# A new table of turns for the two streams of a six-layer decoder kernel

## The chip, the cores and the metric

One core of a Trainium2 chip runs the whole program. The metric is the device time of one execution in microseconds (us), from the first to the last instruction and what the runtime adds around it. The engines of the core are PE (matmul), DVE (vector), ACT (activation), POOL (GpSimd) and SP, which here issues every DMA. Each runs its own list of instructions strictly in the order of the list, and they meet only at semaphores.

## The reference

A batch of 16 sequences of 256 tokens with 256 features goes through six sublayers. Each adds its output to its input and normalises the sum:

```python
x = _layernorm(x + mamba(x))             # L0: scan with 512 channels x 16 states, 256 steps
x = _layernorm(x + sparse_latent(x, ctx))  # L0: 16 heads, 64 chosen keys for each query
x = _layernorm(x + bit_ffn(x))           # L0: quantised feed-forward, 256 -> 1024 -> 256, gelu
x = _layernorm(x + self_attention(x))    # L1: 16 heads of 16
x = _layernorm(x + cross_attention(x, ctx))  # L1: 16 heads of 64
x = _layernorm(x + moe(x))               # L1: 8 experts, top 6, and a shared one
```

The names on the right are short forms of the reference's functions. All is float32; sequences don't depend on each other.

## The kernel before

The sequences are worked one after the other, with two of them in flight. Stream x carries a sequence through mamba, latent attention and the quantised feed-forward layer; stream y carries the sequence ahead of it through self attention, cross attention and the mixture of experts. Both keep their activations in SBUF (`region_x`, `region_y`) and share the eight PSUM banks: 0 to 3 are x's, 4 to 7 are y's.

On each of SP, PE, ACT and DVE the work of a stream is a Python generator; what it emits between two `yield`s is a piece, its waits included. `merged` first emits a number of x pieces, then takes turns from a table: "x2 y1" is two pieces of x, then one of y. One pass through the table is one sequence of each stream, and the table is repeated for all sequences. So the table alone sets in which order an engine's instructions of the two streams stand; the order within a stream never changes. POOL has one stream only and is not in the table.

These are the names that the rows below speak of.

- Where one sequence ends and the next begins. Stream y ends with the last gate products of the experts (L1719, L1723 on DVE), the down projection (L941 on PE, in two halves) and the residual and norm (L1413, L1385 to L1404). The next sequence's self attention transposes x on PE (L467, which needs the residual's read of the bank to be over), ACT copies it (L993), PE projects q and k (L746), DVE copies q (L1642), ACT k (L1174), PE projects v (L753), and then come eight rounds of scores (L609 on PE, maximum L1559 on DVE), a shift (L615, L1567) and scores again for the exponentials (L628 on PE, L1103 on ACT).
- Meanwhile stream x ends its feed-forward layer (L727, L1628, norm) and starts the next mamba: turned counts of chosen keys (L488 on PE, mask on DVE L1462 and L1463, L497 on PE, copy L1469), the clearing of two pads (L1492, L1498), and 32 units of scan. A unit k needs rows broadcast by DMA (L332), a product (L1516 on DVE, every fourth on POOL, L1315), a decay factor (L1062 on ACT, 2 instructions), the scan (L1536 on DVE) and a product on POOL (L1323); every four units PE sums them (L553). ACT may make the factor of unit k only when scan k-2 is over, since two PSUM banks take turns. After the last, DVE gates the result (L1505).
- The feed-forward stretch. Stream x quantises (L1430 to L1432), PE turns the result (L688), ACT copies it (L1128), PE multiplies (L699), DVE scales (L1600) and builds one-hot codes for the next sequence's counts (L1452, two instructions a round). Next to it stream y projects cross attention's output (L861), adds and normalises (L1413 to L1404), and PE transposes the result (L467) for the router and the experts (L870, L880).
- SP issues the broadcast rows and, between them, the big weights: `wide` for the next cross attention (L348), `down` for the experts' down projection (L414) and for cross attention (L422).

Of the kernel before, what the change touches and what calls it, by code (L numbers as in the profile page):

```python
# [37 lines left out]


ORDER = {  # L40
    "sp": (123, "x19 y2 x2 y1 x25 y2 x2 y1 x23"),
    "pe": (60, "x1 y3 x1 y11 x1 y4 x1 y6 x1 y4 x1 y9 x1 y7 x2 y3 x3 y2 x1 y2 x3 y1 x1 y1 x4 y1 x1 y2 x1 y1 x2 y1 x1 "
        "y1 x1 y1 x3 y1 x3 y1 x2 y1 x2 y1 x1 y1 x1 y1 x1 y1 x1 y3 x2 y1 x2 y1 x1 y4 x1 y2 x2 y2 x1 y1 x1 y1 "
        "x2 y1 x3 y1 x2 y2 x1 y1 x1 y1"),
    "act": (80, "y1 x7 y1 x5 y2 x1 y1 x1 y1 x1 y2 x1 y2 x1 y3 x2 y3 x1 y3 x1 y1 x1 y2 x1 y2 x2 y3 x2 y1 x1 y3 x2 y1 "
        "x1 y1 x1 y4 x5 y2 x1 y9 x3 y2 x2 y1 x2 y1 x5 y1 x2 y2 x5 y4 x3 y4 x3 y1 x1 y2 x1 y1 x2 y1 x2 y1 x4 "
        "y1 x2 y1 x2 y1 x2 y1"),
    "v": (141, "y1 x3 y1 x2 y1 x1 y6 x1 y1 x20 y1 x5 y1 x4 y1 x15 y2 x2 y4 x1 y1 x2 y1 x2 y1 x12 y1 x20 y2 x1 y1 x1 "
        "y4 x1 y1 x1 y1 x4 y2 x1 y2 x1 y2 x6 y1 x2 y1 x13"),
}  # L50


# [1822 lines left out]
```

## Time and profile before

| what | value |
|---|---|
| median of three runs | 3820.13 us (3819.62 to 3820.35) |
| span of the profiled execution, first to last instruction | 3818.7 us |
| PE busy | 3224.1 us, 84% of the span |
| DVE busy | 2835.6 us, 74% |
| ACT busy | 2082.8 us, 55% |
| POOL busy | 922.9 us, 24% |
| PE's granted clock, mean over the span | 0.941 |

The profiled span lies 1.4 us below the median. The sixteen sequences repeat the same pattern, so one sequence is read closely, the one that starts near 1600 us. In a timeline a row begins with the start and the duration in us; a bracket at its end says how long the engine stood idle before it and what ended that. PEclk is the granted share of PE's full clock.

### The profile page before, as it was taken

The numbers are of one execution on the slowest core, as the hardware profiler recorded it, in microseconds if no ns is written. First come the engines' busy times: TensorE is split into PE (matmuls) and PEld (weight loads), VectorE is DVE, ScalarE is ACT, GpSimd is POOL, SyncE is SP. The second block draws the span as 40 slices with busy tenths as digits, with TensorE's granted clock in tenths as the row PEclk, the third lists the DMA queues.
The fourth block names the chain that finished last, engine by engine and source line by source line (L and its number), as shares of the span: only waits on it lengthen the run. The fifth ranks groups of instructions, "written<-read, shape, count | busy, mean of one in ns | idle before, by whom it ended". The sixth has DMA issues, their size and how long they took to land.

```text
span 3818.7 us, 59008 instructions
## 1 busy us (share of the span) xinstructions
PE 3224.1 (84%) x22354; PEld 2240.1 (59%) x22402; DVE 2835.6 (74%) x4915; ACT 2082.8 (55%) x4816; POOL 922.9 (24%) x740
## 2 busy tenths in 40 slices
PE   2568989898898989989898998989889898988877
PEld 1245656666565666656566665656656565665655
DVE  4687786868778687877868778786877868687622
ACT  3356655565665656566464655656566565555432
POOL 1423050221404122140411305031230503114000
PEclk8679999999999999999999999999999999999988
DMA  5212141422304142130413213041331404123110
GB/s 187 79 61 92 31 137 47 145 70 79 128 23 148 51 136 78 55 127 33 163 51 127 87 43 138 34 158 57 114 100 31 150 34 152 62 99 109 48 42 17
DMA packets 205692, 336.50 MB, mean 88 GB/s; under 512 B 23968, under 2 KB 175008, under 8 KB 190688
## 3 DMA queue, kind: packets, MB, share of 16 engines
q1 hardware_dynamic: 205408, 332.72, 25.6%
q8 instruction: 177, 2.90, 0.3%
q14 instruction: 107, 0.88, 0.1%
HBM read 311.66 MB, written 20.97 MB: 87 GB/s over the span
## 4 chain that ended last, share of the span: by engine, by line
PE 55%; DVE 23%; ACT 15%; issue 6%; POOL 0%; SPq 0%; DMA 0%; DVEq 0%; ACTq 0%
PE ps L880 7%; PE ps L628 6%; PE ps L609 5%; PE ps L941 4%; DVE nm L1559 3%; PE ps L795 3%; PE ps L781 3%; PE ps L771 3%; PE ps L826 2%; ACT ps L1062 2%; PE ps L640 2%; DVE region_x L1536 2%; PE ps L553 2%; ACT region_y L1211 2%; PE ps L670 2%
## 5 line engine op out<-in xcount | busy, mean ns | idle before, releaser
L1323 POOL TENSOR_TENSOR region_x<-region_x 128x512 f32<-128x512 f32 x512 | 646.8, 1275 | 360.4 <-DVE region_x L1536 359.2
L1536 DVE TENSOR_TENSOR_SCAN region_x<-ps,region_x 128x512 f32<-128x512 f32 x512 | 614.2, 1213 | 76.4 <-ACT ps L1062 76.3
L1062 ACT ACTIVATE ps<-region_x,aneg 128x255 f32<-128x255 f32 x1024 | 440.0, 474 | 326.3 <-DVE region_x L1536 324.1
L1303 POOL TENSOR_TENSOR region_x<-region_x 128x512 f32<-128x512 f32 x96 | 121.7, 1267 | 1195.2 <-ACT region_x L1010 1190.2
L1315 POOL TENSOR_TENSOR region_x<-region_x 128x512 f32<-128x512 f32 x128 | 162.8, 1272 | 1021.4 <-DVE region_x L1516 881.2
L1559 DVE TENSOR_REDUCE nm<-ps 128x4 f32<-128x1024 f32 x256 | 308.0, 1221 | 62.5 <-PE ps L609 56.7
L880 PE MATMUL ps<-xTy,wide 128*128 128x256 f32 x1280 | 331.2, 410 | 1.1 <-DVE region_y L1723 1.1
L1211 ACT ACTIVATE region_y<-ps,rmax 128x256 f32<-128x256 f32 x512 | 235.8, 497 | 126.0 <-DVE rmax L1664 126.0
L880 PEld LDWEIGHTS ps<-xTy,wide 128*128 128x128 f32 x1280 | 251.8, 203 | 47.4 <-issue 8.7
L1664 DVE TENSOR_REDUCE rmax<-ps 128x4 f32<-128x1024 f32 x128 | 152.3, 1220 | 151.2 <-PE ps L807 151.2
L1516 DVE TENSOR_TENSOR region_x<-region_x,ps 128x512 f32<-128x512 f32 x384 | 255.0, 664 | 5.9 <-PE ps L553 5.0
L1572 DVE SCALAR_TENSOR_TENSOR region_x<-region_x,cntk 128x512 f32<-128x512 f32 x256 | 168.4, 690 | 113.9 <-ACT region_x L1103 113.3
L553 PE MATMUL ps<-region_x,sely 128*32 128x256 f32 x2048 | 144.5, 407 | 85.2 <-POOL region_x L1323 85.1
L1227 ACT ACTIVATE region_y<-ps 128x512 f32<-128x512 f32 x256 | 142.3, 599 | 115.1 <-PE ps L829 115.1
L609 PE MATMUL ps<-region_y 64*128 64x256 f32 x1024 | 165.2, 462 | 44.0 <-DVE VP L1649 31.8
L628 PE MATMUL ps<-region_y 64*128 64x256 f32 x1024 | 154.8, 423 | 55.3 <-ACT region_y L1103 42.0
L1103 ACT ACTIVATE region_x<-ps 128x512 f32<-128x512 f32 x256 | 145.3, 605 | 78.0 <-PE ps L628 77.8
L1413 DVE TENSOR_TENSOR xh<-ps,xh 128x512 f32<-128x512 f32 x80 | 54.8, 685 | 170.1 <-PE ps L670 64.5
L1103 ACT ACTIVATE region_y<-ps 128x512 f32<-128x512 f32 x256 | 140.2, 596 | 64.1 <-PE ps L628 63.9
L609 PEld LDWEIGHTS ps<-region_y 64*128 64x128 f32 x1024 | 108.5, 224 | 103.4 <-DVE nm L1559 42.1
L976 ACT ACT_TABLE_LOAD x127 | 162.9, 1283 | 3.0 <-PEq L1865 0.7
L628 PEld LDWEIGHTS ps<-region_y 64*128 64x128 f32 x1024 | 93.4, 197 | 120.5 <-ACT region_y L1103 92.7
(249 smaller groups left out, 6884.6 us busy)
## 6 DMA issues: line engine op xcount, KB each, us to landing
region_x<-rows_of_dt SPq DMA_DIRECT2D x1024, 128.0 KB, 2.9
wide<-in_wgate SPq DMA_DIRECT2D x16, 1280.0 KB, 8.2
wide<-in_wup SPq DMA_DIRECT2D x16, 1280.0 KB, 10.9
down<-in_wmoe SPq DMA_DIRECT2D x16, 1280.0 KB, 7.4
wide<-in_wq SPq DMA_DIRECT2D x16, 1024.0 KB, 5.4
wide<-in_wk SPq DMA_DIRECT2D x16, 1024.0 KB, 7.3
wide<-in_wv SPq DMA_DIRECT2D x16, 1024.0 KB, 9.6
down<-in_wo SPq DMA_DIRECT2D x16, 1024.0 KB, 12.5
```

Source lines behind the costliest of these rows:

```text
L553: last = mm(bank(0)[32 * j:32 * j + 32, m, :], W["sely"][:, e, :], hbuf[(4 * n + j) % HSLOTS][:, half, :], start=(e + half == 0), stop=(e ...
L609: last = mm(ps[:, b + j, qt * T:(qt + 1) * T], a.QT[r, t, qt * P:(qt + 1) * P], a.KT[u % 2][r, t, :], start=not a.masked, stop=not a.maske ...
L628: last = mm(ps[:, a.sT_bank(n + j), kt * T:(kt + 1) * T], a.KT[e][r, t, kt * P:(kt + 1) * P], a.QT[r, t, :], start=True, stop=True)
L880: last = mm(bank(b)[:, j, :], w[:, k, f * P:(f + 1) * P], xTy[:, k, :], start=(k == 0), stop=(k == KD - 1))
L1062: last = f(ps[:, 1 + 2 * (k % 2), half * T + 1:(half + 1) * T], dt_rep[k % SLOTS][:, 1:T], ACT.Exp, scale=aneg[:, k, half:half + 1])
L1103: f(a.PT[:, n % 8].rearrange("p k q -> p (k q)"), ps[:, a.sT_bank(n), :], ACT.Exp).then_inc(a.probs, 1)
L1211: last = f(junk2[:, 4 * (u % 2) + 2 * qt + g], ps[:, a.pair_bank(u) + g, qt * T:(qt + 1) * T], ACT.Exp, bias=rmax[:, qt, g, u:u + 1], accu ...
L1323: nc.gpsimd.tensor_tensor(hbuf[k % HSLOTS], hbuf[k % HSLOTS], csb, ALU.mult).then_inc(hc_ready, 1)
L1516: tt_(hbuf[k % HSLOTS], dtx_rep[k % SLOTS].unsqueeze(1).to_broadcast([P, 2, T]), bank(2), ALU.mult).then_inc(dbx, 1)
L1536: nc.vector.tensor_tensor_scan(flat(hbuf[k % HSLOTS]), ps[:, 1 + 2 * (k % 2), :], flat(hbuf[k % HSLOTS]), 0.0, ALU.mult, ALU.add).then_inc ...
L1559: last = nc.vector.tensor_reduce(at_nm[:, u % 2::2, :, 16 + t], ps[:, b:b + 2, :].rearrange("p g (q k) -> p g q k", k=T), AX, ALU.max, neg ...
L1572: stt(a.PT[:, n % 8], a.PT[:, n % 8], 4.0, cntk[:], ALU.min, ALU.mult).then_inc(a.weighed, 1)
```

## The change

The tables of SP, PE, ACT and DVE are laid out anew, and each stream x gets a somewhat longer start (123 to 140 pieces on SP, 60 to 61 on PE, 80 to 83 on ACT, 141 to 142 on DVE). The pieces, their instructions, their waits and their buffers are the same. Of the diff, SP's line:

```diff
-    "sp": (123, "x19 y2 x2 y1 x25 y2 x2 y1 x23"),
+    "sp": (140, "y1 x1 y1 x10 y1 x16 y1 x3 y1 x2 y1 x39"),
...
```

On SP the load of `down` for the experts (L414) stood right behind the two stores of the scan's first half, and now has seven of the broadcasts (L332) between them and it; the load of `wide` (L348) stands two broadcasts earlier; and `down` for cross attention (L422) three broadcasts behind that of `wide`, which it followed at once.

In the rows of the order below, a matmul of float32 is counted once, where the trace records its two passes, and the scan (L1536) stands as SCALAR_TENSOR_TENSOR. On DVE, where one sequence ends and the next begins, before (the mask, the residual and norm of y, the copy of the counts, the pad, then the scan's first products):

```order
L1463 TENSOR_SCALAR mask<-ps 128x256
L1413 TENSOR_TENSOR xh<-ps,xh 128x512
L1385 BN_STATS y_stats<-xh 128x6 x2
L1387 MEMSET spare 128x1
L1389 BN_AGGR y_mv<-y_stats 128x2 x2
L1469 COPY cntk<-ps 128x512
L1498 MEMSET ps 128x2
L1516 TENSOR_TENSOR region_x<-region_x,ps 128x512
L1397 SCALAR_TENSOR_TENSOR y_nt<-y_mv,y_rstd 128x2
L1398 SCALAR_TENSOR_TENSOR y_nt<-y_nt,y_rstd 128x2
L1399 SCALAR_TENSOR_TENSOR y_rstd<-y_nt,y_rstd 128x2
L1404 TENSOR_SCALAR xh<-xh,y_mv,y_rstd 128x256 x2
```

and now:

```order
L1463 TENSOR_SCALAR mask<-ps 128x256
L1469 COPY cntk<-ps 128x512
L1498 MEMSET ps 128x2
L1516 TENSOR_TENSOR region_x<-region_x,ps 128x512 x2
L1536 SCALAR_TENSOR_TENSOR region_x<-ps,region_x 128x512
L1516 TENSOR_TENSOR region_x<-region_x,ps 128x512
L1536 SCALAR_TENSOR_TENSOR region_x<-ps,region_x 128x512
L1413 TENSOR_TENSOR xh<-ps,xh 128x512
L1385 BN_STATS y_stats<-xh 128x6 x2
L1387 MEMSET spare 128x1
L1389 BN_AGGR y_mv<-y_stats 128x2 x2
L1536 SCALAR_TENSOR_TENSOR region_x<-ps,region_x 128x512
```

The residual of y (L1413) moved from ahead of the first product to behind the second scan, and the small instructions of its norm (L1397 to L1404), which stood behind the first product, now stand further on, behind the seventh scan and just ahead of L1642.

On PE at the same place (L880 and L886 are the experts' products, L479 counts the chosen keys), before:

```order
L886 MATMUL ps<-wT,selx 128x256 x2
L479 MATMUL ps<-region_x 32x16 x32
L941 MATMUL ps<-down,region_y 128x256 x10
L488 MATMUL ps<-identb,region_x 128x32 x16
L941 MATMUL ps<-down,region_y 128x256 x10
L497 MATMUL ps<-identb,cntq 128x128 x4
```

and now:

```order
L880 MATMUL ps<-xTy,wide 128x256 x4
L479 MATMUL ps<-region_x 32x16 x32
L886 MATMUL ps<-wT,selx 128x256 x2
L488 MATMUL ps<-identb,region_x 128x32 x16
L941 MATMUL ps<-down,region_y 128x256 x10
L497 MATMUL ps<-identb,cntq 128x128 x4
L941 MATMUL ps<-down,region_y 128x256 x10
```

The turning of the counts (L488, L497) moved ahead of each half of the down projection (L941), where it stood behind each. On ACT the decay factors of units 0 to 2 (L1062) now stand ahead of the y norm's L988 and of L993, behind which they stood.

In the feed-forward stretch on PE, as a piece of the difference:

```order
 L840 MATMUL ps<-region_y 64x256 x12
 L688 MATMUL ps<-identb,region_x 128x128 x4
-L861 MATMUL ps<-down,region_y 128x256 x8
-L699 MATMUL ps<-w1q,region_x 128x512 x8
+L699 MATMUL ps<-w1q,region_x 128x512 x4
+L861 MATMUL ps<-down,region_y 128x256 x8
+L699 MATMUL ps<-w1q,region_x 128x512 x4
 L861 MATMUL ps<-down,region_y 128x256 x8
 L503 MATMUL ps<-xTx,win 128x256 x8
```

The first half of the x stream's multiplication (L699) moved ahead of the first half of y's projection (L861). On DVE there, before:

```order
L1600 SCALAR_TENSOR_TENSOR region_x<-ps,small,region_x 128x1024 x2
L1452 TENSOR_TENSOR region_x<-region_x,iota 128x1024
L1452 TENSOR_TENSOR region_x<-region_x,iota 128x512
L1413 TENSOR_TENSOR xh<-ps,xh 128x512
L1385 BN_STATS y_stats<-xh 128x6 x2
L1387 MEMSET spare 128x1
L1389 BN_AGGR y_mv<-y_stats 128x2 x2
L1397 SCALAR_TENSOR_TENSOR y_nt<-y_mv,y_rstd 128x2
```

and now:

```order
L1600 SCALAR_TENSOR_TENSOR region_x<-ps,small,region_x 128x1024 x2
L1413 TENSOR_TENSOR xh<-ps,xh 128x512
L1385 BN_STATS y_stats<-xh 128x6 x2
L1387 MEMSET spare 128x1
L1389 BN_AGGR y_mv<-y_stats 128x2 x2
L1397 SCALAR_TENSOR_TENSOR y_nt<-y_mv,y_rstd 128x2
L1398 SCALAR_TENSOR_TENSOR y_nt<-y_nt,y_rstd 128x2
L1399 SCALAR_TENSOR_TENSOR y_rstd<-y_nt,y_rstd 128x2
L1404 TENSOR_SCALAR xh<-xh,y_mv,y_rstd 128x256 x2
L1452 TENSOR_TENSOR region_x<-region_x,iota 128x1024
L1452 TENSOR_TENSOR region_x<-region_x,iota 128x512
```

The residual and norm of y moved ahead of a round of one-hot codes (L1452). On other places the table moves single pieces: a round of maxima of x (L1559) ahead of one of y (L1664), sums of four units (L553) behind a neighbour, and in the scans' second half the decay factors (L1062) by up to three pieces later among y's exponentials and copies, with y's residual and norm after self attention together and ahead of scans 20 and 21.

## Rows read from the trace of the kernel before

**Rows 1.** The page: span, chain, two groups (busy us, mean ns | idle), one load.

```profile
span 3818.7 us, 59008 instructions
...
PE 55%; DVE 23%; ACT 15%; issue 6%; POOL 0%; SPq 0%; DMA 0%; DVEq 0%; ACTq 0%
...
L1536 DVE TENSOR_TENSOR_SCAN region_x<-ps,region_x 128x512 f32<-128x512 f32 x512 | 614.2, 1213 | 76.4 <-ACT ps L1062 76.3
...
L1516 DVE TENSOR_TENSOR region_x<-region_x,ps 128x512 f32<-128x512 f32 x384 | 255.0, 664 | 5.9 <-PE ps L553 5.0
...
down<-in_wmoe SPq DMA_DIRECT2D x16, 1280.0 KB, 7.4
```

**Rows 2.** Stretches: from:to, us, busy PE PEld DVE ACT POOL, PEclk, DMA share, GB/s.

```profile
1622.00:1630.00 8.00, 2.74 (x22) 1.41 (x21) 8.00 (x12) 6.08 (x15) 6.82 (x6) 0.82 0.89 320
...
1774.00:1782.00 8.00, 5.48 (x20) 4.43 (x21) 7.52 (x20) 4.95 (x10) 3.80 (x3) 0.79 0.00 0
```

**Rows 3.** Timeline of PE where sequences meet: start, us, instruction, [idle before <-releaser].

```profile
1602.57 4.55 PE L941 MATMUL ps<-down,region_y 128*128 128x256 f32 x20 [0.52 <-DVE region_y L1723]
...
1619.20 3.62 PE L746 MATMUL ps<-xTy,wk 128*128 128x256 f32 x16
...
1626.46 1.30 PE L553 MATMUL ps<-region_x,sely 128*32 128x256 f32 x16 [3.64 <-POOL region_x L1323]
...
1629.38 3.78 PE L753 MATMUL ps<-wv,xTy 128*128 128x256 f32 x8 [1.62 <-DVE region_y L1642]
...
1649.75 1.14 PE L628 MATMUL ps<-region_y 64*128 64x256 f32 x8 [0.80 <-DVE region_y L1567]
...
1854.65 1.65 PE L753 MATMUL ps<-wv,xTy 128*128 128x256 f32 x3 [1.65 <-DVE region_y L1642]
```

**Rows 4.** Timeline of DVE, the same stretch.

```profile
1612.78 0.69 DVE L1413 TENSOR_TENSOR xh<-ps,xh 128x512 f32<-128x512 f32 x1 [1.35 <-PE ps L941]
...
1615.95 1.12 DVE L1399 SCALAR_TENSOR_TENSOR y_rstd<-y_nt,y_rstd 128x2 f32<-128x2 f32 x1
...
1627.45 1.87 DVE L1642 TENSOR_SCALAR region_y<-ps,hmq,qbh 128x256 f32<-128x256 f32 x4
...
1634.70 1.23 DVE L1559 TENSOR_REDUCE nm<-ps 128x4 f32<-128x1024 f32 x1 [2.15 <-PE ps L609]
...
1648.50 1.20 DVE L1567 TENSOR_TENSOR region_y<-region_y,ps 128x1024 f32<-128x1024 f32 x1
```

**Rows 5.** Timeline of ACT and of POOL, the same stretch.

```profile
1614.57 0.29 ACT L988 ACTIVATE y_lnv<-y_mv,epsc 128x2 f32<-128x2 f32 x1 [8.99 <-DVE y_mv L1389]
...
1615.78 1.27 POOL L1315 TENSOR_TENSOR region_x<-region_x 128x512 f32<-128x512 f32 x1 [59.96 <-DVE region_x L1516]
```

**Rows 6.** Timeline of SP's queue, the same stretch.

```profile
1591.86 0.45 SPq L414 DMA_DIRECT2D down<-in_wmoe  x1
...
1592.81 5.25 SPq L332 DMA_DIRECT2D region_x<-rows_of_dt  x8
```

**Rows 7.** Timeline of DVE, end of the scans.

```profile
1690.96 1.23 DVE L1536 TENSOR_TENSOR_SCAN region_x<-ps,region_x 128x512 f32<-128x512 f32 x1 [2.01 <-ACT ps L1062]
...
1699.26 0.88 DVE L1505 SCALAR_TENSOR_TENSOR ps<-region_x,dp,ps 128x256 f32<-128x256 f32 x2 [2.67 <-PE ps L553]
```

**Rows 8.** Timeline of PE, the feed-forward stretch.

```profile
1776.92 5.36 PE L861 MATMUL ps<-down,region_y 128*128 128x256 f32 x16
...
1787.30 3.62 PE L503 MATMUL ps<-xTx,win 128*128 128x256 f32 x16
...
1791.41 0.66 PE L467 MATMUL ps<-ident,xh 128*128 128x128 f32 x4 [0.49 <-DVE xh L1404]
```

**Rows 9.** Timeline of DVE, the feed-forward stretch.

```profile
1783.55 2.47 DVE L1600 SCALAR_TENSOR_TENSOR region_x<-ps,small,region_x 128x1024 f32<-128x1024 f32 x2
...
1785.94 1.82 DVE L1452 TENSOR_TENSOR region_x<-region_x,iota 128x1024 bf16<-128x1024 bf16 x2
...
1787.67 0.68 DVE L1413 TENSOR_TENSOR xh<-ps,xh 128x512 f32<-128x512 f32 x1
```

16 rows, old and new, of the table ORDER are left out of this document.

## The prediction

> **What bounds the kernel now.** I read the chain of waits first: 55% of it is PE, 23% DVE, 15% ACT [rows 1]. No engine bounds the whole; PE leads, and hands over in places. Then I looked for where PE stands idle, and what its neighbours do there. The pattern repeats: L753 of one sequence starts at 1629.38, of the next at 1854.65 [rows 3], so a period is 225.3 us. Both streams run side by side in 15 periods (16 sequences, y one behind x); what the table saves in one counts 15 times. The lone start of x and the lone end of y stay.
>
> Two stretches are not PE's. The first is where sequences meet. PE waits 3.64 before L553 and 1.62 before L753 [rows 3], is busy 2.74 of 8 us while DVE is busy all 8.00, and is granted 0.82 of its clock [rows 2]. The price of that clock is seen too: L753's 8 passes took 3.78 us, L746's 16 of the same width 3.62 [rows 3]. DVE works through from the residual L1413 at 1612.78 and waits for PE only at the end, 2.15 us before the first maximum L1559 [rows 4]. ACT had waited 8.99 us for y's norm with the scan's factors queued behind it [rows 5].
>
> The second is the feed-forward stretch: clock 0.79 [rows 2], L861's 16 passes in 5.36 us where L503's 16 took 3.62, and L467 waits for y's norm [rows 8], which on DVE stands behind a pair of one-hots [rows 9].
>
> **Where sequences meet.** The same instructions run, so only waits change. PE first. Of the 5.66 us between the end of L941's first half (1607.12) and L1413, the second half takes 4.55 [rows 3, 4], so L488 takes 1.1. It now stands ahead of the first half, which moves from 1602.6 to about 1603.9. It ends at 1608.4, and then L497 waits for the mask. Now the mask is done at 1611.4 (L1413's start less its 1.35 of waiting, rows 4). In the new order x's residual no longer stands behind the last gate products, and I estimate the mask 1.1 earlier, 1610.3 (bounds: not earlier at all, or 2 earlier, when L497 would not wait). PE so stands some 1.9 us, the second half ends at 1615.2, and L1413 comes at 1615.3, 2.5 later than now.
>
> In exchange DVE has something to do before it: three products and two scans, 3 x 0.66 + 2 x 1.21 = 4.4 us [rows 1], for ACT makes their factors ahead of y's norm. From L1413 to the first L1559 it is 21.9 us now [rows 4]. Of that go the 2.15 of waiting, the 4.4 already done and 0.5 for the count's copy and pad; two products and a scan (2.5) come in, moved up from between the maxima. That makes 17.3, and L1559 at 1632.6. PE may be a little later than that: L1642 would end near 1628.2, and L753 at the low clock (3.78) and a first round of L609 give 1633.5. I take 1632.9, which is 1.8 earlier. From there to L1567 it is 13.8 us now; of the 2.5 that left, I count 1.3, since PE's rounds hid the rest. L1567, which L628 waits for [rows 3], comes 3.1 us earlier; I enter -3.0. The bounds are -4.5 (no low clock, mask 2 earlier) and +2.4 (first rival).
>
> SP: L414 goes behind seven broadcasts, 7 x 5.25/8 = 4.6 us after 1592.8 [rows 6]; with its 7.4 to landing [rows 1] it lands at 1604.8 at the latest, 0.9 after L941 wants it, while its own transfer would be shorter without the broadcasts behind it. I enter +0.3 (0 to +0.9). The loads of `wide` go out some 5 us earlier; 3 MB at the 320 GB/s of this stretch [rows 2] is 10 us, so the broadcast for product 10, now behind them, lands near 1629, and DVE wants it near 1631: nothing. The store of y's result waits for a later norm; what SP holds behind it are broadcasts for unit 13 and on, wanted 20 us later: nothing.
>
> **The scans' second half.** y's residual and norm now precede scans 20 and 21, and twelve scans must run close together to be in time. There is a little room: the last gate L1505 waits 2.67 us for PE's sum, and one scan waited 2.01 for its factor [rows 7]. Twelve scans and eight products are 12 x 1.21 + 8 x 0.66 = 19.8 us, less than the 24.7 that they take now with the norm and these waits between. I enter +0.4 (0 to +2.5, every such wait as now).
>
> **The feed-forward stretch.** L1600 ends at 1786.0, the one-hots take 1.8, and L1413 follows at 1787.67 [rows 9]. Behind the norm instead of ahead of it, they give L467 1.8 us, and L1600 itself may come 0.4 earlier, since x's projection is no longer behind a y piece: up to -2.2. But L503 must be through PE before L467, and it waits for L1600: now 1787.30 to 1790.92 [rows 8], then from 1785.6 to 1789.2. Ahead of it PE would stand about 2.5 us, which here goes with the low clock: L861's 5.36 against 3.62 puts L503's end back by 1.7 to 1790.9. So it is -2.2 or -0.5; both clocks occur in this stretch, and I take the middle, -1.4 (bounds -2.2 and 0). The earlier L699 fills an idle PE and is not late: its reader L1600 stands behind the digits on DVE in any case. The single moves that are left (maxima, sums of four, one-hots by a place) I enter as nothing, -0.5 to +0.3: PE is busy beside them.
>
> Sum per period: -3.0 + 0.3 + 0.4 - 1.4 = -3.7; times 15 is -55.5. From the span of 3818.7 that gives 3763.2, and with the 1.4 by which the median of the runs lies above it 3764.6, say 3765.
>
> **The rivals.** *Slower: y's norm meets POOL.* The two-column L1399 took 1.12 us, from 1615.95 to 1617.07, and POOL's product ended at 1617.05 [rows 4, 5]: it stood until POOL was through. In the new order the five small instructions L1397 to L1404 stand just ahead of L1642, when POOL has the scans' products to do, 1.27 each. If each waits for one, that is 6.4 us in place of the 1.0 now, +5.4 on L1642, and with the other terms +1.7 a period: 3846. From four such waits on (+4.1) the kernel is slower, with three (+2.8) it is not. Against it: POOL should itself be waiting then, for unit 11's broadcast behind `wide`.
>
> The Trainium skill (SBUF — State Buffer, section "SBUF: two separate sides") states this as a lock: a VectorE instruction with two SBUF inputs or in a two-port mode and a GpSimd instruction take the shared ports in turn, and the second is blocked for the whole of the first. The trace agrees in the one case above; by the rule all five could be held, and the sum would be that 3846.
>
> *The clock falls in L941.* PE's new stand of 1.9 us lies in the middle of L941. Waits of 1.62 and 3.64 went with the low clock [rows 2, 3]. If it falls there as it does in L861, the second half takes 1.7 more and L1413 with it: -2.0 a period, 3790. At the worst, all of the half at the low clock, it is +4.5, which makes 3832.
>
> *The gain is given back by the scans.* If the twelve scans wait for factors as now, +2.5 in place of +0.4: -1.6 a period, 3796. For it speaks that ACT's factors stand up to three pieces later; against it the room in front of L1505.
>
> **How the numbers follow.** The forecast (3765, its own range 3735 to 3790) has 0.55, the clock 0.15, the scans 0.13, POOL 0.12, and 0.05 is left for PE being the bound after all, without a change. A difference under 0.2%, 7.6 us, can't be told from none. Faster: 0.54 + 0.12 + 0.10 = 0.76; same: 0.01 + 0.02 + 0.02 + 0.04 = 0.09; slower: 0.01 + 0.01 + 0.12 + 0.01 = 0.15. The range goes from 3728 (-6.1 a period, the good ends of the terms) to 3825, which leaves out most of the POOL case and little else.
>
> **What would show it.** A period of about 221.5 us from L753 to L753. Scans 0 and 1 ahead of L1413, and L1413 later in its period by 2 to 3 us, counted from L727. A wait of PE before L497 of about 2 us. L1567 some 3 us earlier. L414's landing not what L941 waits for. In the feed-forward stretch L1413 right behind L1600, and L503 waiting for L1600. L1505 still waiting for PE rather than for POOL or ACT. I am wrong if small instructions of y's norm take over 1 us each ahead of L1642, if L941's second half takes 6 us or more, or if the period is 225 or longer.

## The result, and the profile after

The changed kernel took 3785.27 us (median of four runs, 3781.05 to 3788.39) against 3820.24 of before. The ratio is 0.9905, with an interval of 0.9892 to 0.9917: faster, 35 us where 55 were forecast, and inside the range of 3728 to 3825.

The page after [rows 1], and the line of the load that the prediction had priced at 0.3:

```profile
span 3785.4 us, 59056 instructions
...
PE 52%; DVE 22%; ACT 15%; issue 5%; DMA 3%; SPq 1%; POOL 0%; DVEq 0%; ACTq 0%
...
L1536 DVE TENSOR_TENSOR_SCAN region_x<-ps,region_x 128x512 f32<-128x512 f32 x512 | 615.9, 1214 | 32.1 <-ACT ps L1062 29.9
...
L941 PE MATMUL ps<-down,region_y 128*128 128x256 f32 x640 | 174.2, 436 | 37.2 <-DMA down<-in_wmoe 34.3
...
down<-in_wmoe SPq DMA_DIRECT2D x16, 1280.0 KB, 7.2
```

DMA stood at 0% of the chain of waits and has 3% now. The scans wait less for their factors, 32.1 instead of 76.4 us, but the experts' down projection L941 waits 34.3 us for its weights, in 13 of its 16 times. That is new: in before it waited only for the gate product L1723 [rows 3].

One period of after on PE, from the start of the feed-forward's second multiplication (L727), from which all times of a period are counted below; in before the row that answers to it is the second fence:

```profile
2027.79 1.91 PE L727 MATMUL ps<-w2q,region_x 128*128 128x256 bf16 x16
...
2042.93 7.18 PE L941 MATMUL ps<-down,region_y 128*128 128x256 f32 x20 [3.83 <-DMA down<-in_wmoe]
2049.95 0.39 PE L497 MATMUL ps<-identb,cntq 128*128 128x128 bf16 x4
2050.18 4.54 PE L941 MATMUL ps<-down,region_y 128*128 128x256 f32 x20
...
2067.66 1.99 PE L753 MATMUL ps<-wv,xTy 128*128 128x256 f32 x8
```

```profile
1592.07 1.91 PE L727 MATMUL ps<-w2q,region_x 128*128 128x256 bf16 x16
```

L941 starts 15.1 us into the period (10.5 in before), after 3.83 of waiting, and its first half takes 7.18 instead of 4.55 [rows 3]: part of it runs at the low clock. The window of that half, with the columns of [rows 2], has a granted clock of 0.63:

```profile
2043.00:2050.00 7.00, 7.00 (x21) 5.58 (x22) 2.53 (x7) 0.87 (x2) 0.00 (x0) 0.63 0.55 185
```

SP's queue says why it waits:

```profile
2029.94 4.44 SPq L332 DMA_DIRECT2D region_x<-rows_of_dt  x7
2034.42 0.59 SPq L414 DMA_DIRECT2D down<-in_wmoe  x1
```

The load goes out 6.6 us into the period, where before issued it 0.2 ahead of L727 [rows 6]. DVE in the same period [rows 4], with POOL beside the small instructions:

```profile
2054.96 0.67 DVE L1413 TENSOR_TENSOR xh<-ps,xh 128x512 f32<-128x512 f32 x1
...
2064.30 0.34 DVE L1397 SCALAR_TENSOR_TENSOR y_nt<-y_mv,y_rstd 128x2 f32<-128x2 f32 x1
2064.67 0.16 DVE L1398 SCALAR_TENSOR_TENSOR y_nt<-y_nt,y_rstd 128x2 f32<-128x2 f32 x1
2064.86 0.16 DVE L1399 SCALAR_TENSOR_TENSOR y_rstd<-y_nt,y_rstd 128x2 f32<-128x2 f32 x1
...
2084.09 1.22 DVE L1567 TENSOR_TENSOR region_y<-region_y,ps 128x1024 f32<-128x1024 f32 x1 [0.53 <-PE ps L615]
```

```profile
2063.34 1.27 POOL L1323 TENSOR_TENSOR region_x<-region_x 128x512 f32<-128x512 f32 x1 [0.43 <-DVE region_x L1536]
2067.84 1.27 POOL L1315 TENSOR_TENSOR region_x<-region_x 128x512 f32<-128x512 f32 x1 [3.23 <-DMA region_x<-rows_of_dt]
```

L1413 comes 27.2 into this period instead of 20.7, and L1567 at 56.3 instead of 56.4: DVE made up for the delay and hardly more. The feed-forward stretch ahead of it [rows 8]:

```profile
1990.49 1.04 PE L699 MATMUL ps<-w1q,region_x 128*128 128x512 bf16 x4 [1.21 <-ACT region_x L1128]
1991.36 3.62 PE L861 MATMUL ps<-down,region_y 128*128 128x256 f32 x16
...
1999.13 3.62 PE L503 MATMUL ps<-xTx,win 128*128 128x256 f32 x16
2003.08 0.66 PE L467 MATMUL ps<-ident,xh 128*128 128x128 f32 x4 [0.33 <-DVE xh L1404]
```

```profile
1999.33 0.69 DVE L1413 TENSOR_TENSOR xh<-ps,xh 128x512 f32<-128x512 f32 x1 [1.27 <-PE ps L861]
```

Here L861's first half is at the full clock (granted 1.00 from 1984 to 1992), 3.62 instead of 5.36, and DVE waits 1.27 for its second half before L1413.

The periods differ from each other, so the table has means over eleven of them (the fourth to the fourteenth), from the start of L727, worked out from the timelines; down_early and before_boundary are experiments below. The last row adds up the stretches in which the granted clock was half.

| us after L727 | before | after | down_early | before_boundary |
|---|---|---|---|---|
| L941 starts | 10.5 | 13.9 | 11.2 | 11.2 |
| L941's second half ends | 20.7 | 25.4 | 22.6 | 22.6 |
| L1413 starts | 20.7 | 25.6 | 22.9 | 22.9 |
| L1567 starts | 56.1 | 55.2 | 53.2 | 53.5 |
| L795 ends | 105.2 | 104.0 | 101.5 | 102.4 |
| L870 starts | 200.9 | 198.4 | 195.9 | 198.7 |
| next L727 | 225.2 | 222.4 | 219.8 | 221.7 |
| low clock in a period | 17.4 | 14.3 | 9.0 | 13.7 |

After against before by stretches: up to L1567 -0.85, from there to L795's end -0.4, to L870 -1.2, to the next L727 -0.4, together -2.8. The last of these is the clock: in before the way from L870 to the next L727 takes 24.45 us in the ten periods with 3.4 us of low clock in it and 23.02 in the one without, in after 23.22 where the clock stays full. The thirteen middle periods gain 36.7; the start of x is 1.7 longer, the first and the last period 0.9 together and the end of y 0.8: 33.3, the difference of the spans.

### The profile page after: what moved, and what is told of

The parts are those of the page before. It is cut to its first block, busy times and chain, and to the rows that moved or that the text cites. A ratio compares the mean times of both kernels' runs of the same rounds, so it can differ in the third digit from the quotient of the medians.

```text
span 3785.4 us, 59056 instructions
## 1 busy us (share of the span) xinstructions
PE 3217.3 (85%) x22402; PEld 2235.2 (59%) x22402; DVE 2812.2 (74%) x4915; ACT 2086.8 (55%) x4816; POOL 923.3 (24%) x740
## 4 chain that ended last, share of the span: by engine, by line
PE 52%; DVE 22%; ACT 15%; issue 5%; DMA 3%; SPq 1%; POOL 0%; DVEq 0%; ACTq 0%
PE ps L609 6%; PE ps L628 6%; PE ps L795 3%; PE ps L861 3%; PE ps L771 3%; PE ps L781 3%; DVE nm L1559 3%; PE ps L746 3%; PE ps L941 3%; PE ps L553 3%; DMA down<-in_wmoe 3%; DVE region_x L1536 2%; PE ps L640 2%; PE ps L826 2%; PE ps L605 2%
## 5 line engine op out<-in xcount | busy, mean ns | idle before, releaser
L1536 DVE TENSOR_TENSOR_SCAN region_x<-ps,region_x 128x512 f32<-128x512 f32 x512 | 615.9, 1214 | 32.1 <-ACT ps L1062 29.9
L1062 ACT ACTIVATE ps<-region_x,aneg 128x255 f32<-128x255 f32 x1024 | 445.1, 472 | 309.0 <-DVE region_x L1536 178.2
L1559 DVE TENSOR_REDUCE nm<-ps 128x4 f32<-128x1024 f32 x256 | 308.7, 1223 | 63.6 <-PE ps L609 53.4
L880 PE MATMUL ps<-xTy,wide 128*128 128x256 f32 x1280 | 323.2, 405 | 0.5 <-DVE region_y L1723 0.5
L880 PEld LDWEIGHTS ps<-xTy,wide 128*128 128x128 f32 x1280 | 250.4, 201 | 42.6 <-issue 5.7
L1572 DVE SCALAR_TENSOR_TENSOR region_x<-region_x,cntk 128x512 f32<-128x512 f32 x256 | 167.1, 690 | 115.9 <-ACT region_x L1103 114.0
L1664 DVE TENSOR_REDUCE rmax<-ps 128x4 f32<-128x1024 f32 x128 | 152.2, 1220 | 132.9 <-PE ps L807 132.9
L1413 DVE TENSOR_TENSOR xh<-ps,xh 128x512 f32<-128x512 f32 x80 | 55.0, 687 | 210.9 <-PE ps L670 104.6
L941 PE MATMUL ps<-down,region_y 128*128 128x256 f32 x640 | 174.2, 436 | 37.2 <-DMA down<-in_wmoe 34.3
L609 PE MATMUL ps<-region_y 64*128 64x256 f32 x1024 | 153.5, 435 | 59.0 <-DVE VP L1649 34.4
L628 PE MATMUL ps<-region_y 64*128 64x256 f32 x1024 | 157.5, 430 | 41.2 <-ACT region_y L1103 36.2
L553 PE MATMUL ps<-region_x,sely 128*32 128x256 f32 x2048 | 146.4, 409 | 44.0 <-POOL region_x L1323 44.0
L941 PEld LDWEIGHTS ps<-down,region_y 128*128 128x128 f32 x640 | 139.5, 222 | 62.3 <-DMA down<-in_wmoe 35.6
L840 PE MATMUL ps<-region_y 128*64 128x256 f32 x1024 | 137.3, 394 | 35.7 <-ACT region_y L1201 34.9
```

The source lines that it names most:

```text
L553: last = mm(bank(0)[32 * j:32 * j + 32, m, :], W["sely"][:, e, :], hbuf[(4 * n + j) % HSLOTS][:, half, :], start=(e + half == 0), stop=(e ...
L609: last = mm(ps[:, b + j, qt * T:(qt + 1) * T], a.QT[r, t, qt * P:(qt + 1) * P], a.KT[u % 2][r, t, :], start=not a.masked, stop=not a.maske ...
L628: last = mm(ps[:, a.sT_bank(n + j), kt * T:(kt + 1) * T], a.KT[e][r, t, kt * P:(kt + 1) * P], a.QT[r, t, :], start=True, stop=True)
L880: last = mm(bank(b)[:, j, :], w[:, k, f * P:(f + 1) * P], xTy[:, k, :], start=(k == 0), stop=(k == KD - 1))
L941: last = mm(bank(7)[:, tt, :], mhT[:, f, tt * P:(tt + 1) * P], wmoe[:, f, :], start=(n == 0), stop=(n == KM - 1))
L1062: last = f(ps[:, 1 + 2 * (k % 2), half * T + 1:(half + 1) * T], dt_rep[k % SLOTS][:, 1:T], ACT.Exp, scale=aneg[:, k, half:half + 1])
```

## The experiments

All give a ratio to before, run beside it; differences in us between two experiments compare runs that were made at different times. The edits are fragments of the table's lines.

**down_early.** SP's load back ahead of the broadcasts, all else as after.

```diff
-    "sp": (140, "y1 x1 y1 x10 y1 x16 y1 x3 y1 x2 y1 x39"),
+    "sp": (140, "y1 x1 y1 x3 y1 x23 y1 x3 y1 x2 y1 x39"),
```

> The kernel after, with the load of down for the experts (L414) back where before has it, behind the two stores and ahead of the seven broadcasts. Theory (the load's landing is the whole miss): in the kernel after, L941 waits 2.6 us a period for the load, and its first half then runs 6.1 to 7.6 us instead of 4.55; in the one period where the load came in time, the second half ended 22.6 us after L727's start instead of 25.4 on average. So all periods do as that one: L497 waits about 2.0 for the mask, L1567 comes 2.8 earlier, the period is 219.6, the time 3746 (3738 to 3758). Rival, the clock: once L941 no longer waits ahead of its first half, the wait before L497 drops the clock in its second half, 6.2 instead of 4.5: 1.1 gained a period, 3769. Rival, given back: L1413 is earlier, but DVE's scans or later waits absorb it: 3778 to 3787.

3744.49 us, ratio 0.9792 (0.9776 to 0.9808): 41 us better than the change (43 by the two ratios), and the fastest version here. One period on PE:

```profile
1557.22 1.91 PE L727 MATMUL ps<-w2q,region_x 128*128 128x256 bf16 x16
...
1568.46 4.58 PE L941 MATMUL ps<-down,region_y 128*128 128x256 f32 x20
1575.06 0.40 PE L497 MATMUL ps<-identb,cntq 128*128 128x128 bf16 x4 [2.01 <-DVE mask L1463]
1575.29 4.54 PE L941 MATMUL ps<-down,region_y 128*128 128x256 f32 x20
```

No wait for the load, 4.58 for the first half, a stand of 2.01 before L497, and 4.54 for the second half: the clock did not fall behind that stand. The second half took 4.54 in every period, and no period waited for the load. The first theory holds, both rivals fall. One thing it did not have: in three of the eleven periods the first half went at the low clock all the same (granted 0.73), with no wait for the load ahead of it:

```profile
2007.40 6.27 PE L941 MATMUL ps<-down,region_y 128*128 128x256 f32 x20
2013.99 0.40 PE L497 MATMUL ps<-identb,cntq 128*128 128x128 bf16 x4 [0.32 <-DVE mask L1463]
2014.22 4.54 PE L941 MATMUL ps<-down,region_y 128*128 128x256 f32 x20
```

There it cost nothing, for PE then stood 0.32 instead of 2.01 before L497. What lowered the clock in these three stays open.

**before_down_late.** The reverse: before, with the load behind the seven broadcasts.

```diff
-    "sp": (123, "x19 y2 x2 y1 x25 y2 x2 y1 x23"),
+    "sp": (123, "x19 y2 x9 y1 x18 y2 x2 y1 x23"),
```

> The kernel before, with L414 moved behind the seven broadcasts, as the kernel after has it, and nothing else. Theory: the load goes out 4.6 us later, lands about 12.2 us after L727's start (7.4 after its issue), L941 wants it at 10.5 and waits 1.7 to 3; its first half then goes at the low clock, 1.7 to 2.6 more; L1413 follows at once, so 3.5 to 5.5 a period, 3875 to 3900. Rival (the prediction's step): the load hides but for 0.3 a period: 3825.

3914.92 us, ratio 1.0222 (1.0194 to 1.0249): 90 us slower, more than expected. Its group of waits for L941:

```profile
  DMA down<-in_wmoe: 53.3, 14
```

That is 3.8 each time; the first half then took 6.2 to 7.6. L1567 starts at 61.3 instead of 56.1 and the next L727 at 231.8 instead of 225.2: 5.2 of the 6.6 a period are lost where the load is, as expected, and most of the rest in the scans' second half at a low clock. In before no first half of L941 was slow; here, with the load's place as the only edit, all were.

**down_middle.** As down_early, with four broadcasts ahead of the load.

```diff
-    "sp": (140, "y1 x1 y1 x10 y1 x16 y1 x3 y1 x2 y1 x39"),
+    "sp": (140, "y1 x1 y1 x7 y1 x19 y1 x3 y1 x2 y1 x39"),
```

> As down_early, but L414 behind four broadcasts instead of none (in the kernel after it is seven). Theory: it goes out 2.6 us later, lands at 11 to 12.5 us after L727, where L941 wants it at 11.2; a wait of up to 1 us, with a slower first half behind it, still fits mostly into the 2.0 us that PE stands before L497 in any case: 3744 to 3762. Rival: each broadcast ahead of the load costs the same, 41 us for seven: 3767.

3756.27 us, ratio 0.9838 (0.9816 to 0.9859). L941 waited in nine of the periods, 10.2 us in all, where the kernel after had 34.3; most of it went into the 2.0 that PE stands anyhow. Four of the seven broadcasts cost 12 of the 41 us. By the ratios it is 18 of 43, and the interval just reaches the 25 that proportion asks for; the trace decides it: L941's second half ends at 23.1, against 22.6 in down_early and 25.4 in after, 0.5 of 2.8. So it is not in proportion.

**early_L497_behind.** As down_early, with L488 and L497 behind the halves of L941, as in before.

```diff
-"... y1 x4 y1 x1 y1 x1 y1 x1 y1 x1 y1"
+"... y1 x4 y1 x1 y1 x1 y2 x1 y1 x1"
```

> As down_early, but the two halves of L941 one place earlier on PE: L488 and L497 stand behind each half, as before has them. Theory: L497 in between is what gives DVE its three products and two scans while PE works the second half. With L497 behind, the counts come at about 21 us after L727, DVE does these 4.9 us and only then L1413, at 25.6 instead of 23: the gain of down_early is lost, 3780 to 3787. Rival: DVE works through the same list anyway and the place of L497 changes nothing: 3746, as down_early.

3780.76 us, ratio 0.9886 (0.9871 to 0.9902), as the theory had it:

```profile
1820.99 0.42 DVE L1469 COPY cntk<-ps 128x512 bf16<-128x512 bf16 x1 [3.32 <-PE ps L497]
...
1825.58 0.67 DVE L1413 TENSOR_TENSOR xh<-ps,xh 128x512 f32<-128x512 f32 x1
```

```profile
1826.30 1.12 PE L467 MATMUL ps<-ident,xh 128*128 128x128 f32 x4 [5.35 <-DVE xh L1413]
```

DVE idles 3.32 us for L497, and PE then 5.35 for L1413, which has DVE's products and scans ahead of it. DVE's new order pays only with PE's.

**before_boundary.** Before, with the first and last turns of PE, ACT and DVE as in the change, and SP as before.

```diff
-    "v": (141, "y1 x3 y1 x2 y1 x1 y6 x1 y1 x20 ... y2 x1 y2 x1 y2 x6 y1 x2 y1 x13"),
+    "v": (142, "y1 x5 y1 x1 y3 x1 y5 x19 ... y3 x3 y1 x1 y2 x11 y1 x9 y1"),
```

> The kernel before with the change's moves where sequences meet, on PE, ACT and DVE, and nothing else; SP's table is that of before, so that the load of down (L414) goes out ahead of the broadcasts. Theory: with the load in time this is the prediction's first term alone. L497 waits 2.0 for the mask, L941's second half ends 22.6 after L727, L1567 comes 2.9 earlier; nothing behind it gives back: period 222.3, 3777 (3768 to 3790). Rival: the gain rests on the moves behind it (scans' second half, feed-forward), without which the scans wait for their factors or PE's clock falls behind L1567: 3795 to 3815.

3774.07 us, ratio 0.9873 (0.9856 to 0.9889): 47 us, close to the prediction's first term (-3.0 in 15 periods, 45), and more than the whole change with its late load. That it is so close is partly luck. L1567 comes 2.6 a period earlier. The other 0.9 goes with the clock: from L870 to the next L727 it is 1.3 shorter, with no low clock there (23.03, as before's own period without it), the feed-forward stretch is 0.65 longer, with more low clock, and the way between L1567 and L795's end is 0.3 shorter, since one period of before has low clock there and none here.

**before_ffn.** Before, with y's norm ahead of the one-hots on DVE, and the first half of L699 ahead of L861.

```diff
-    v:  "... y1 x12 y1 x20 y2 x1 y1 x1 y4 ..."
+    v:  "... y1 x12 y1 x19 y2 x2 y1 x1 y4 ..."
-    pe: "... y3 x2 y1 x2 y1 x1 y4 ..."
+    pe: "... y3 x3 y1 x1 y1 x1 y4 ..."
```

> The kernel before with the feed-forward part of the change alone: on DVE y's residual and norm (L1413, L1397 to L1404) ahead of the last pair of one-hots, and on PE the first half of L699 ahead of L861. Theory: 1.3 to 1.4 us a period, as the prediction's term and the comparison of the two traces have it (L870 comes 2.46 earlier, of which 1.1 was gained earlier): 3800 (3796 to 3806), period 223.9. Rival: the stretch gains only because what goes before it comes earlier: 3817 to 3821.

3865.89 us, ratio 1.0107 (1.0093 to 1.0121): 41 us slower, and both readings miss. The feed-forward stretch on PE:

```profile
1797.18 0.36 PE L688 MATMUL ps<-identb,region_x 128*128 128x128 bf16 x2 [2.53 <-DVE region_x L1432]
...
1799.18 1.89 PE L699 MATMUL ps<-w1q,region_x 128*128 128x512 bf16 x4 [0.69 <-ACT region_x L1128]
1800.86 5.21 PE L861 MATMUL ps<-down,region_y 128*128 128x256 f32 x16
```

PE still waits 2.53 before L688, and behind it L699 (1.89 for the 1.04 of after) and L861 (5.21) are at the low clock (granted 0.58 from 1796 to 1804). With L699 ahead of L861 the projection starts later, and L1413, now ahead of the one-hots, waits for it: the stretch from L795's end to L870 is 97.04 us in ten of eleven periods instead of 95.57. More is lost elsewhere. Ten us from the start of L628 on, in before_ffn and then in before:

```profile
1667.00:1677.00 10.00, 8.21 (x42) 4.34 (x44) 8.10 (x10) 6.58 (x15) 6.96 (x7) 0.53 0.25 75
```

```profile
1649.00:1659.00 10.00, 7.47 (x72) 4.28 (x72) 10.00 (x12) 8.59 (x20) 8.91 (x8) 1.00 0.32 104
```

The columns are those of [rows 2]. Up to L1567 both kernels keep step within half a microsecond (56.08 and 56.07 us on the mean, 56.0 and 56.4 in most periods), the order here is the same, and yet the granted clock is 0.53 in one and 1.00 in the other; a block of L628 takes 2.0 instead of 1.14, and the scans end 3.6 later. That is so in ten of the eleven periods, where before has it in one. So an edit in one stretch changed the clock in another that it doesn't touch.

**before_lat_end, before_lat_ffn, early_no_ffn.** The single moves at the end of latent attention alone; the same and before_ffn's; and down_early without before_ffn's. The first, against before:

```diff
-    pe:  "... y1 x2 y1 x1 y1 x1 y1 x1 y1 x1 y3 x2 ..."
+    pe:  "... y1 x2 y1 x3 y2 x1 y4 x2 ..."
-    act: "... x3 y2 x2 y1 x2 y1 x5 y1 x2 y2 x5 y4 x3 y4 x3 ..."
+    act: "... x3 y2 x4 y1 x1 y1 x2 y1 x4 y2 x4 y1 x1 y1 x2 y1 x1 y4 x2 y1 x1 ..."
-    v:   "... x2 y1 x12 y1 x20 y2 ..."
+    v:   "... x2 y1 x10 y1 x22 y2 ..."
```

The last line puts one product of y on DVE (L1676) two of x's products (L1572) earlier, which the expectation doesn't name.

> The kernel before with only the single moves at the end of latent attention (PE: L503, L670 ahead of the last L840; ACT: the order of the last copies around the convolution's products), which the prediction entered as nothing. Theory from the trace of after: they split PE's wait of 2.53 ahead of L688 into shorter ones, after which L861's first half runs 3.62 at the full clock instead of 5.36; L503, L1600 and the norm come 1.0 to 1.7 earlier: 3797 to 3806. Rival: they are nothing (the prediction), and the gain is in the norm's place on DVE: 3816 to 3823.

> The kernel before with the moves at the end of latent attention and those of the feed-forward stretch together. If the clock of L861 is the gain: L861 3.62 and 3.62, as before_lat_end or up to 0.5 a period better, 3793 to 3806. If the norm's place on DVE is the gain and the clock has no part in it: 3798 to 3802 while before_lat_end shows no gain. If the slow L628 phase that the feed-forward moves alone brought (L628 at 2.0 us) comes again: 3830 or more.

> As down_early, but with the norm's place on DVE (L1413 to L1404 behind the pair of one-hots) and the first half of L699 (behind L861) as in before. If L861's clock is the gain of the stretch and comes from the moves ahead of it: 3743 to 3752. If the norm's place is: 1.3 a period lost, 3764.

3828.45 us (1.0017, 1.0008 to 1.0026), 3810.87 (0.9968, 0.9956 to 0.9979) and 3764.12 (0.9839, 0.9803 to 0.9874). The first two meet none of their readings; the third meets that of the norm's place, but its runs lie between 3742.52 and 3777.33. So the whole times don't settle the question, but the stretch from L795's end to L870 does. It takes one of a few lengths, by the moves that are in it and by how long the granted clock is low in it:

| us from L795's end to L870 | clock full | 3.4 us low | 6.8 us low |
|---|---|---|---|
| before, before_boundary | | 95.57 | 96.40 to 96.61 |
| before_down_late | 95.59 | 95.58 | 96.69 |
| before_lat_end, early_no_ffn | 95.04 | 96.74 | |
| before_ffn | | 96.23 | 97.04 |
| before_lat_ffn, after, down_early | 94.42 | | |

With both parts it was at the full clock in all eleven periods. The moves at the end of latent attention gain 0.5 where the clock stays full, the norm's place another 0.6 on top of them, and without them the clock is low and the norm's place loses. L861's clock alone is not the gain: before_down_late has before's order in this stretch, and in two of its periods L861 went at the full clock, and still the stretch took 95.57 and 95.59:

```profile
2045.41 0.29 PE L688 MATMUL ps<-identb,region_x 128*128 128x128 bf16 x2 [2.53 <-DVE region_x L1432]
...
2046.45 3.67 PE L861 MATMUL ps<-down,region_y 128*128 128x256 f32 x16
```

With y's norm behind the one-hots, DVE is what L467 waits for [rows 8, 9], and an earlier L861 gives nothing. Rows of before_lat_end, then DVE in before_lat_ffn:

```profile
1781.62 3.69 PE L861 MATMUL ps<-down,region_y 128*128 128x256 f32 x16 [1.78 <-ACT region_y L1201]
...
1794.27 0.66 PE L467 MATMUL ps<-ident,xh 128*128 128x128 f32 x4 [0.33 <-DVE xh L1404]
```

```profile
1784.54 0.69 DVE L1413 TENSOR_TENSOR xh<-ps,xh 128x512 f32<-128x512 f32 x1 [1.25 <-PE ps L861]
```

In the first, L861 is at the full clock (granted 1.00 from 1781 to 1785), and what is left is DVE's norm; in the second, DVE waits for PE. That before_lat_end is slower as a whole comes from the L628 phase: in five of its eleven periods the clock is low there, and these take 228.1 us; the six others take 222.7 to 224.7.

**before_sp_rest, before_scans.** SP's other moves alone, and the moves in the scans' second half alone (on ACT too, as in the change).

```diff
-    sp: (123, "x19 y2 x2 y1 x25 y2 x2 y1 x23")
+    sp: (123, "x17 y1 x1 y1 x3 y1 x23 y1 x3 y1 x2 y1 x22")
...
-    v:  "... y1 x20 y1 x5 y1 x4 y1 x15 y2 ..."
+    v:  "... y1 x20 y3 x24 y2 ..."
```

> The kernel before with all moves of the change on SP except that of L414: the loads of wide (L348) two broadcasts earlier, wo2 (L422) and the store of y's result later, the loads of the next context and of the experts' wide one and two places earlier. The prediction entered all of them as nothing: 3816 to 3824. Rival: the broadcasts held behind them make the scans wait: over 3828.

> The kernel before with the change's moves in the scans' second half alone (y's residual and norm ahead of scans 20 and 21, ACT's decay factors later among y's exponentials and copies). The prediction's term is +0.4 a period: 3826. From the traces (L567 to L1505 took 16.5 in before, 15.4 to 15.9 where these moves are in, 16.2 with the moves where sequences meet alone) it is -0.3 to -0.8: 3808 to 3816. A third reading: the difference is the clock behind L567 and not the order, then it may lie on either side, within 10 us of before.

The L567 of this expectation is L1567. 3821.15 us (0.9998, 0.9989 to 1.0008) and 3819.54 (0.9998, 0.9987 to 1.0009). SP's other moves are nothing that can be told from the noise, as predicted. The scans' part is nothing as a whole, as the third reading had it, but two things in its parts: from L1567 to L795's end eight periods take 48.16 us, where before takes 48.82 in ten, and three take 52.03, with the clock low for 10.2 us behind L1567 (in before one, 52.43). So the order gains 0.65, and the clock gave it back.

## Why the prediction was right, and where it was not

**Where sequences meet: right.** With the load in time (down_early), L941 starts at 11.2, PE stands 2.0 before L497 (forecast 1.9), the second half ends at 22.6 (23.1) and L1413 starts at 22.9 (23.2). L1567 comes 2.9 earlier (3.1). Alone (before_boundary) the moves give 2.6 at L1567; that the whole is 47 us for 45 owes something to where the clock fell.

**The step that failed is SP's: "I enter +0.3 (0 to +0.9)".** Counted from L727, the sum had the load go out at 5.3 (4.6 behind 1592.8), land at 12.7 at the latest and be wanted at 11.8. On the mean of the eleven periods it went out at 6.4, L941 started with it at 13.9, and with the load in time it starts at 11.2. So the landing is 1.2 later than the latest that I counted, for the stores of the scan's rows, and with them the broadcasts ahead of the load, begin 1.4 later in the period; and L941 wants it 0.6 earlier. I also entered less than the 0.9 that I had counted, in the hope of a shorter transfer without broadcasts behind it. The runs show no such thing for certain: the median from issue to landing is 7.4 in before and 7.6 in before_down_late, and 8.1 in down_early against 7.2 in after, each pair differing in the load's place alone. The Trainium skill (DMA: Bandwidth & Descriptors, section "Queues, rings and completion order") says that a DMA engine consumes descriptors in the order of their ring, though a later one may finish first. By that order what is queued behind the load would not delay it: the first pair agrees, the second does not, and it stays open. And the term had no price for the clock: PE waits 2.6 on average, and the first half then takes 6.7 instead of 4.55. Of these 4.8 go the 2.0 before L497, which PE needn't stand any more: 2.8 at the end of L941, 2.6 a period, 41 us on the chip.

With +2.6 for +0.3 the sum is -1.4 a period, where after has -2.8. The difference is in what I had entered too high, and down_early shows it without the load: -2.9 for -3.0 where sequences meet, -0.85 for +0.4 in the scans' second half, -1.2 for -1.4 in the feed-forward stretch and -0.45 for nothing from L870 on, together -5.4 for -4.0. In the total another error stands against that: I counted 15 periods, but the gain came in thirteen (36.7 us), and the first and the last period and the two ends lost 3.4. These errors partly cancel, and that is luck.

**The scans' second half and the way from L870 on.** In the first +0.4 was forecast; -0.65 is what the order does where the clock stays full. The second I had not entered; it came 0.4 shorter, by less low clock and not by the order.

**The feed-forward stretch: the size right by luck, the way not.** -1.4 was forecast, -1.2 came. But two signs did not come: L1413 does not start right behind L1600 but waits 1.27 for L861, and L503 follows L861 at once and does not wait for L1600. I priced the norm's place and L699's, and entered the moves ahead of them as nothing. What I priced loses 41 us alone, 1.3 a period of it in this stretch. It needs the others: with them PE's wait of 2.53 before L688 is gone, 1.21 before L699 is left, and L861 goes at the full clock, for which DVE waits in the new order. That the wait is what lowers the clock is argued and not shown: behind the same wait the clock stayed full in two of eleven periods of before_down_late.

**The parts don't add up.** 47, 10, 3 and 1 us alone make 61, while down_early, which has them all, gains 80 on its own runs of before. (The 3 and the 1 are within the noise, and a round of maxima, L1559 ahead of L1664, is in down_early and in no part.) The larger parts alone lost to the clock somewhere: before_boundary 0.83 in the feed-forward stretch in ten periods of eleven, before_lat_ffn and before_scans 3.6 to 3.9 behind L1567 in three, where before itself has one. Order and clock can be counted apart here because in one kernel a stretch repeats, with few exceptions, to 0.05 us at the same amount of low clock.

**The rivals.** *POOL*: L1397 took 0.34 and ended with POOL's product, the next two 0.16, since POOL then stood 3.23 for a broadcast, as argued; these three durations are the same in all periods. The rule of the Trainium skill (SBUF — State Buffer, section "SBUF: two separate sides") fits the one that was held; five such waits didn't come. *The clock in L941*: it fell in the first half, behind the wait for the load, and not behind the stand before L497. It also fell there without that wait (three periods of down_early), where it cost nothing. *Given back by the scans*: no, they wait less, 32.1 us in all instead of 76.4.

## What to carry to other kernels

When a table moves work ahead, follow each load to its landing from the same anchor as its reader, with what its queue now has ahead of it, and price a new PE wait with the slower matmuls that may follow it: here 2.6 us of waiting came with 2.1 of slower matmuls. A part measured alone can mislead where a second part removes the wait behind it; test the pair. Before a change is judged as a whole, take out its worst single piece: here one load's place was worth more than the whole change.

## What the runs showed that was not expected

The clock's share can move with no instruction near it moved. In before_ffn the same order, within half a microsecond of the same times after L727, got 0.53 of the clock behind L1567 where before got 1.00, worth 3.6 us of a period. before_ffn does so in ten of eleven periods, others in three or five; before itself in one (19.81 us from L1567 to L1505 where its others take 16.20). What decides it stays open: no run here moved the clock alone. So an effect of about 1% of this kernel can be the clock's place and not the order.
